# The local pass of a graph network with each product as one full fp32 matmul in place of three on rounded parts

## The reference

```python
def _gcn_conv(x, W, b, src, dst, dinv):
    h = x @ W
    norm = dinv[src] * dinv[dst]
    agg = segment_sum(h[src] * norm[:, None], dst, n)
    agg = agg + (dinv * dinv)[:, None] * h
    return agg + b

x = _l2norm(_gcn_conv(node_embedding, W1, b1, ...))        # 128 -> 256
def f(z):
    z1 = _l2norm(_gcn_conv(z, Wf1, bf1, ...))              # 256 -> 256
    return _gcn_conv(z1, Wf2, bf2, ...) + z                # 256 -> 256
k1 = f(x); k2 = f(x + 0.5 * k1); k3 = f(x + 0.5 * k2); k4 = f(x + k3)
x = x + (k1 + 2.0 * k2 + 2.0 * k3 + k4) / 6.0
x = _gcn_conv(x, W2, b2, ...)                              # 256 -> 128
```

## Time and profile before

| | |
|---|---|
| median of the runs | 7418.31 us |
| the profiled execution, its span | 7463.9 us |
| the local pass in it | 249 to 2481 us |
| busy over the whole span | PE 84%, DVE 82%, POOL 65%, ACT 51% |
| mean granted TensorE clock | 0.938 of full speed |

### The profile page before, as it was taken

The page is one execution under the profiler, slowest core; times in us unless marked ns, Lnnn a source line. Parts: engine busy times, 40 slices in busy tenths (PEclk is TensorE's granted clock), DMA queues, the critical chain, the costliest instruction groups (busy, mean ns, idle before and its releaser), DMA issues. The chain is left out here.

```text
span 7463.9 us, 156875 instructions
## 1 busy us (share of the span) xinstructions
PE 6262.2 (84%) x37260; PEld 5197.7 (70%) x37260; DVE 6114.0 (82%) x15796; ACT 3838.3 (51%) x10696; POOL 4840.9 (65%) x5469
## 2 busy tenths in 40 slices
PE   7699889899999657989989998999888765877776
PEld 3588888888889436867766676667666554865664
DVE  8588778787888777889879977997799887878887
ACT  6466666666666576733661166116622233654443
POOL 0488888888873576855776577657744565546665
PEclk8799999999999899999999999999999998988998
DMA  0365555554444466879779977997799765543432
GB/s 2 102 165 161 161 160 158 162 161 152 146 145 152 146 190 199 247 257 297 229 223 332 329 226 224 331 327 228 230 385 387 259 186 151 152 138 119 125 123 86
DMA packets 981268, 1483.74 MB, mean 199 GB/s; under 512 B 156967, under 2 KB 450705, under 8 KB 980647
## 3 DMA queue, kind: packets, MB, share of 16 engines
q1 hardware_dynamic: 685479, 922.39, 37.2%
q0 software_dynamic: 141504, 309.42, 16.2%
q10 hardware_dynamic: 153664, 244.12, 9.0%
HBM read 902.58 MB, written 573.11 MB: 198 GB/s over the span
## 5 line engine op out<-in xcount | busy, mean ns | idle before, releaser
L1336 PE MATMUL bank<-c_rows,sums_all 128*128 128x256 f32 (+1 forms) x3920 | 1320.9, 420 | 550.5 <-DVE c_rows L1487 304.3
L751 PE MATMUL bank<-wf_w,c_xt 128*128 128x256 f32 x6272 | 1615.0, 381 | 2.0 <-DVE y L1545 2.0
L1381 ACT ACTIVATE c_xt<-bank 128x512 f32<-128x512 f32 (+1 forms) x980 | 556.8, 568 | 1586.6 <-issue 831.0
L1307 POOL DMA_INDIRECT c_rows<-t_tab,src_pair x784 | 870.2, 1110 | 705.6 <-PE bank L1336 546.2
L1336 PEld LDWEIGHTS bank<-c_rows,sums_all 128*128 128x128 f32 x3920 | 633.9, 194 | 984.7 <-DVE c_rows L1487 478.7
L751 PEld LDWEIGHTS bank<-wf_w,c_xt 128*128 128x128 f32 x6272 | 1133.7, 191 | 127.0 <-ACT c_xt L1381 3.5
L1487 DVE SCALAR_TENSOR_TENSOR c_rows<-bank,carry,c_rows 32x256 f32<-32x256 f32 (+1 forms) x1950 | 913.7, 469 | 274.3 <-PE bank L1336 117.6
L1307 POOL DMA_INDIRECT c_rows<-z_tab,src_pair x784 | 770.7, 983 | 293.3 <-issue 189.5
L1085 DVE TENSOR_TENSOR lx_lo<-bank,lx_hi 128x512 fp32r<-128x512 f32 (+1 forms) x1000 | 658.6, 659 | 260.6 <-ACT lx_hi L1030 217.4
L1030 ACT ACTIVATE lx_hi<-bank 128x512 fp32r<-128x512 f32 (+1 forms) x1000 | 569.4, 572 | 580.4 <-PE bank L999 418.6
L741 PE MATMUL bank<-wf_hi,lx_hi 128*128 128x256 f32 x3200 | 725.0, 309 | 62.7 <-issue 49.4
(11 more groups left out here) (333 smaller groups left out, 14629.2 us busy)
## 6 DMA issues: line engine op xcount, KB each, us to landing
c_z<-z_tab SPq DMA_DIRECT2D x882, 256.0 KB
z_tab<-lz SPq DMA_DIRECT2D x400, 256.0 KB
t_tab<-lt SPq DMA_DIRECT2D x400, 256.0 KB
z_tab<-y ACTq DMA_DIRECT2D x392, 256.0 KB
c_own<-z_tab SPq DMA_DIRECT2D x392, 256.0 KB
t_tab<-y ACTq DMA_DIRECT2D x392, 256.0 KB
c_own<-t_tab SPq DMA_DIRECT2D x392, 256.0 KB
fl_x<-x_tab SPq DMA_DIRECT2D x396, 128.0 KB
```

The source lines that it names most:

```text
L751: last = nc.tensor.matmul(out, x(k), w[:, k, :], start=(k == 0), stop=(k == ks - 1 and not bias))
L1307: pool.indirect_dma_start(out=rows[:, s, i, 0:win], out_offset=None, in_=source, in_offset=bass.IndirectOffsetOnAxis(ap=m["src_i"][:, t:t ...
L1336: nc.tensor.matmul(psum[s % 2][:, i * win:(i + 1) * win], sums[:, j * 2 + i, :], rows[:, s, i, 0:win], start=True, stop=True).then_inc(S[" ...
L1381: nc.scalar.activation(xt[:, s % 2].rearrange("p k n -> p (k n)")[:, 0:n], psum[2 + s % 2][:, 0:n], ACT.Copy).then_inc(S["copied"], 1)
```

## The change

`low`, `x_lo`, `w_hi` and `w_lo` go. ACT copies the transposed block unrounded to one buffer `x_t`, at the place of `high`, and PE multiplies it with the unrounded weights by `full_product`: one fp32 matmul where three on fp32r stood. The bias of the end layers stays an fp32r matmul. PE waits for `copied` where it waited for `high` and `low`.

```diff
-        for name, ks, width in (("w1", 1, H2), ("wf1", 2, H2), ("wf2", 2, H2), ("w2", 2, D)):
-            early(name + "_hi", [P, ks, width], F32R)
-            early(name + "_lo", [P, ks, width], F32R)
...
-                for n, (name, ks, width, _) in enumerate(parts):
-                    last = nc.scalar.activation(m[name + "_hi"][:, 0:ks, :], m[name + "_w"][:], ACT.Copy)
...
-                for n, (name, ks, width, _) in enumerate(parts):
-                    nc.vector.tensor_tensor(m[name + "_lo"][:, 0:ks, :], m[name + "_w"][:],
-                                            m[name + "_hi"][:, 0:ks, :].bitcast(F32), ALU.subtract)
...
-        x_hi = sb("lx_hi", [P, 4, 2, H2], F32R)
-        x_lo = sb("lx_lo", [P, 4, 2, H2], F32R)
+        x_t = sb("lx_t", [P, 4, 2, H2])
...
                     if prev:
-                        pe.wait_ge(S["low"], ph.at("low", *prev))
+                        pe.wait_ge(S["copied"], ph.at("copied", *prev))
...
-                    pe.wait_ge(S["high"], ph.at("high", b, q))
-                    pe.wait_ge(S["low"], ph.at("low", b, q))
+                    pe.wait_ge(S["copied"], ph.at("copied", b, q))
...
-                        last = product(nc, psum[4 + n][:, i * width:(i + 1) * width],
-                                       lambda k: x_hi[:, n, k, i * P:(i + 1) * P],
-                                       lambda k: x_lo[:, n, k, i * P:(i + 1) * P],
-                                       m[w + "_hi"], m[w + "_lo"], ks,
-                                       (m["ones_r"], m["bf2_parts"]) if kind[c] == "end" else None)
+                        last = full_product(nc, psum[4 + n][:, i * width:(i + 1) * width],
+                                            lambda k: x_t[:, n, k, i * P:(i + 1) * P], m[w + "_w"], ks,
+                                            (m["ones_r"][:], m["bf2_parts"][:]) if kind[c] == "end" else None)
...
-                staggered(act, blocks, Q, early, [(0, high), (6, scale), (1, begin_rest), (4, square)])
+                staggered(act, blocks, Q, early, [(0, copy), (6, scale), (1, begin_rest), (4, square)])
...
-                staggered(dve, blocks, Q, early, [(6, normalise), (1, low), (3, add_rest), (3, take), (0, build)])
+                staggered(dve, blocks, Q, early, [(6, normalise), (3, add_rest), (3, take), (0, build)])
```

More of the change, by code:

```diff
@@ L704, in _ @@
             def _(act):
-                act.wait_ge(S["weights_in"], 64)
-                for n, (name, ks, width, _) in enumerate(parts):
-                    last = nc.scalar.activation(m[name + "_hi"][:, 0:ks, :], m[name + "_w"][:], ACT.Copy)
-                last.then_inc(S["w_hi"], 1)
                 act.wait_ge(S["biases_in"], 64)
@@ L714, in _ @@
                 dve.wait_ge(S["weights_in"], 64)
-                dve.wait_ge(S["w_hi"], 1)
                 dve.wait_ge(S["biases_in"], 64)
                 nc.vector.tensor_scalar(not_one[:], m["ident"][:, 1:2], -1.0, 1.0, ALU.mult, ALU.add)
-                for n, (name, ks, width, _) in enumerate(parts):
-                    nc.vector.tensor_tensor(m[name + "_lo"][:, 0:ks, :], m[name + "_w"][:],
-                                            m[name + "_hi"][:, 0:ks, :].bitcast(F32), ALU.subtract)
                 nc.vector.tensor_scalar(m["ones_r"][:], m["ident"][:], 0.0, 1.0, ALU.mult, ALU.add)
@@ L733, in _ @@
                                                b_rest[:], ALU.mult, ALU.add)
[L736 to L745, removed]
 def full_product(nc, out, x, w, ks, bias=None):
@@ L818, in local_pass @@
         rates = {
-            "turned": one, "high": one, "low": one, "product": one, "taken": one,
+            "turned": one, "copied": one, "product": one, "taken": one,
             "rest_set": [[0, 0, 0, 0, 1, 0, 1, 0, 3, 1][layer[q]] for q in range(Q)],
@@ L1022, in _, with copy @@
             def _(act):
-                def high(b, q, odd):
+                def copy(b, q, odd):
                     n = H2 if layer[q] == 0 else 2 * H2
@@ L1029, in high @@
                         act.wait_ge(S["product"], ph.at("product", *prev))
-                    nc.scalar.activation(x_hi[:, k].rearrange("p k n -> p (k n)")[:, 0:n], psum[k][:, 0:n],
-                                         ACT.Copy).then_inc(S["high"], 1)
+                    nc.scalar.activation(x_t[:, k].rearrange("p k n -> p (k n)")[:, 0:n], psum[k][:, 0:n],
+                                         ACT.Copy).then_inc(S["copied"], 1)
                 def begin_rest(b, q, odd):
@@ L1079, in normalise @@
                     last.then_inc(S["done"], 1)
[L1081 to L1087, removed]
                 def bias(name, width):
```

## The result

| | before | changed |
|---|---|---|
| median of the runs, us | 7418.31 | 7492.99 (2 runs, 7491.93 to 7494.04) |
| ratio, 95% interval | | 1.0099 [1.0081, 1.0118] |
| profiled execution, span | 7463.9 | 7489.8 |
| local pass in it, us | 249 to 2481 | 247 to 2548 |

The changed kernel is 1.0% slower, 75 us; that is less than the 2% from which this kernel's times are called slower, but clear of the noise. The forecast was 7544, +126, so the change cost 0.6 of what was forecast. The two profiled spans differ by only 26 us, since before's profiled execution was 0.6% above its median and this one is at its own; most of the excess lies behind the pass, where the kernels are the same (4983 us against 4942).

A forecast was written before the change was run, and what follows sets the result against it. POOL and PE were taken to bound the local pass in turn: +5.5 us a period over 21.8 periods gives +120, +11 behind the edge tables, -5 for weights, filling and draining: +126, 7418 to 7544, range 7400 to 7625.

The forecast's parts named there:

- The product: PE's fp32 product in place of three fp32r ones: 0.29 us more per mid or end step, to 2.16 and 2.40.
- rival 3: Four passes at the old price: records of 0.24 us, +92 us more, 7636; chance 0.06.
- Steps 8 to 30: PE's stretch of a period without cover: +6.2 us, 44.0 to 50.2.
- Step 30 to the gather: From PE's step 30 to POOL's next gather: POOL's lag and ACT's wait given back, -0.7 us, 8.4 to 7.7.
- The gather to PE's step 8: POOL's stretch of 36.3 us a period: PE's 2.5 us more work covered by POOL, cost nothing.
- DVE's relief: Removing 1000 `low` instructions, 658.6 us, from DVE buys nothing while the edge tables run.
- Rival 1: Gather to step 8 paced by PE behind DVE's `normalise`; freed PE returns 6 us there: 7400 to 7440; chance 0.17.
- Behind the tables: Last 3 periods, without edge tables: from 81.2 us to PE's own work, at least 84.5; +11 in all.
- Rival 2: Nothing given back: gather stays tied to PE's step 33, POOL's stretch takes PE's 2.5 us: 7633; chance 0.12.
- rival 4: PE with fewer idle gaps keeps clock 1.00 instead of 0.95 over the pass; changes nothing, no share of its own.

The follow-up runs named there:

- e2: Changed kernel with DVE's `low` subtraction put back, its result unread, and PE's products waiting for it: 7556.6 us, ratio 1.0186.
- e5: Changed kernel with POOL's eight edge-table DMAs of steps 28 to 35 moved to steps 12 to 27: 7464.8 us, ratio 1.0057 to before.
- e6: Kernel before with POOL's eight edge-table DMAs of steps 28 to 35 moved to steps 12 to 27: 7506.3 us, ratio 1.0116.
- experiment 3: Asked what slows POOL's own work; kernel before with one of DVE's three residual sums of layer 8 in place of three: 7379.0 us, ratio 0.9947.
- e1: Changed kernel with DVE's `low` subtraction put back, its result unread and PE's products not waiting for it: 7526.1 us, ratio 1.0147 to before.
- e8: Kernel before with `normalise` on DVE moved from lag 6 to lag 9: 7418.1 us, ratio 0.9997.
- e14: Kernel before with one of DVE's three residual sums of layer 8 in place of three, `low` kept: 7379.0 us, ratio 0.9947.
- e3: Kernel before without `low`, its third product taking `x_hi` again with the same 12 matmuls: 7379.7 us, ratio 0.9950.

## Why the prediction was right and where it missed

- **The product** (+0.29 a mid or end step): right, 2.16 and 2.40 us as the coupled stages' rows gave it. Four passes at the old price, rival 3, would have put the records 0.24 apart; they are 0.216.
- **Steps 8 to 30** (+6.2, to 50.2): 49.97 measured, right in size, by luck: two errors against each other. PE's work there grew by 5.5, 43.68 to 49.14 in e2, since before's first turns after step 8 were longer than the 1.87 and 2.11 that I took: the transposes of the kernel before stood 2.17 and 1.99 apart there. And 0.8 us came on top as waits behind step 8 (0.56 of them at step 9), because PE now arrives early.

```profile
1043.19 0.66 PE L999 MATMUL bank<-ident,lt 128*128 128x128 f32 x4
...
1045.36 0.60 PE L999 MATMUL bank<-ident,lz 128*128 128x128 f32 x4
...
1047.35 0.66 PE L999 MATMUL bank<-ident,lt 128*128 128x128 f32 x4
```

- **Step 30 to the gather** (-0.7, to 7.7): 7.80, right.
- **The gather to PE's step 8** ("I cost it at nothing, covered by POOL", 36.3): this is the term that was mis-sized. The means show that it fell from 36.85 to 34.68 (the 36.3 was one period's), 2.2 us a period, 47 us in 21.8, of the 51 us by which the forecast was high; 6.5 us more come from behind the tables, and the other two terms took back 4. That POOL bounds the stretch was right; e5 and e6 show it. Two things were hidden in it. First, 0.9 us of POOL's own instructions were stretched by DVE's sums (experiment 3): "nothing of POOL's own is removed" was true of the list, not of the durations. Second, 1.3 us lay between POOL's inverse and PE's step 8, 2.28 us where 0.98 do: PE came late from its products, which waited for `low`. I had taken that chain (inverse, ACT, PE) as fixed without measuring it against the same chain where PE is idle. That the wait for `low` makes this part is shown by e1 and e2; why `low` is late there is shown only in part (e8).
- **DVE's relief** ("buys nothing with the edge tables running"): wrong for the same reason. It is worth 64 us with the new product and 39 with the old, of which 13 and 18 behind the tables. The share itself came as forecast, 52% of the pass for near 50.
- **Rival 1**, that freeing PE from `normalise` returns 6 us: its direction appeared, at a third of its size. The cause that it named has a part in it: with `normalise` moved (e8) PE's step 8 comes earlier in 12 of 18 periods, but the time stays. It does not reach into POOL's stretch, which DVE's sums lengthen (e14).
- **Behind the tables** (at least 84.5): 82.7. A last product, 128 wide, takes 0.89 us and not 1.34: the 0.17 a record of the earlier trace rows held the switch to the next group of matmuls, and the eight records alone are 0.11 apart. Four times 0.45 is the 1.8 that is missing. Its weight is small, 3 periods.
- **Rival 2** (nothing given back, 7633) and **rival 4** (the clock): the first stretch took none of PE's extra work. The mean clock over the pass rose from 0.95 to 0.98 and moved the time by nothing that the period does not already hold.

## What to carry to other kernels

Where two in-order engines bound a loop in turn, cost each stretch by its own chain, and measure every link against a place where the engine that follows is idle: a link that is longer than there has a third engine's wait in it. Before an engine's stretch is called its own, compare its small instructions with the same ones elsewhere; if they are longer beside another engine's work, relief of that engine shortens the stretch. And when a stretch is bound by a periodic side job, spread the job evenly over the turns in which its engine is idle: that moved this kernel more (133 us) than the change of its arithmetic (75 us). And before a gap or a slow clock is charged to the time, look at the next step: if it starts no later than in a period without them, they cost nothing.

## What the runs showed of the hardware

- A GpSimd instruction on two numbers per partition takes 0.22 us undisturbed and 0.60 on average beside a VectorE instruction with two SBUF operands; beside one with a PSUM and an SBUF operand, 0.24. The power (L905) goes from 0.72 to 0.91 on average, the issue of an indirect DMA (L663) from 1.06 to 1.18.
- An fp32 matmul 256 wide costs 0.43 us (two records of 0.216), three fp32r matmuls 0.36: 1.2 times as much. At 128 wide a record takes 0.11, so 0.22 for one fp32 matmul, where three fp32r ones (0.112 each, in the last products before) take 0.34: narrow products gain by the change, wide ones lose.
- 2.07 us without work ahead of step 8 left TensorE at a granted clock of 0.54 for the next 2.85 us (e3); 1.75 us in the changed kernel left it at 1.00. The length of that gap alone doesn't decide it. In e8, 1.59 us of idle stand ahead of the first of these two stretches of 4 us and 2.03 ahead of the second (columns as in the earlier trace rows; the clock is 0.58 and 1.00):

```profile
669.67:673.67 4.00, 3.99 (x21) 3.99 (x22) 2.52 (x7) 4.00 (x14) 2.98 (x6) 0.58 0.47 164
1025.43:1029.43 4.00, 3.29 (x26) 3.05 (x26) 2.84 (x7) 4.00 (x14) 2.97 (x5) 1.00 0.52 164
```
